# Gated cross-attention and mixture of experts: order of the last maximum, the second products, the selections, a send and a gather at the joint of the two halves

## The reference, cut to what matters

```
x (2, 512, 128), ctx (2, 154, 128), 16 heads of 8
x = x + tanh(g_xattn) * attention(layernorm(x), ctx, ctx)   # causal: query q sees keys k <= q
x = x + tanh(g_ffn)   * moe(layernorm(x))

moe: probs = softmax(xt @ Wr)                # 1024 tokens, 8 experts
     topv, topi = top_k(probs, 2);  topv = topv / sum(topv)
     rank = cumsum(onehot(topi), axis=0)     # per choice and expert, in token order
     keep = (rank <= 160) * onehot           # capacity of an expert for each choice
     h = gelu(xt @ W1[e] + b1[e]);  y = h @ W2[e] + b2[e]    # 128 -> 512 -> 128
     out = sum over e of w[t, e] * y[e, t]
```

## Time and profile before

| | us |
|---|---|
| median of 3 runs | 141.88 (141.72 to 141.99) |
| the profiled execution | 142.43 |
| its span, first to last instruction | 140.2 |
| busy: PE, DVE, POOL, ACT | 122.2, 103.5, 83.6, 74.1 |

### The profile page before, as it was taken

One profiled execution on the slowest core, in us unless ns is written; L12 is line 12 of the kernel. 1 busy time (PEld: TensorE's weight loads), 2 busy tenths in 40 slices (PEclk: granted clock), 3 DMA queues, 4 the chain that ended last, 5 costly groups with the idle time before them and its releaser, 6 DMA issues.

```text
span 140.2 us, 2215 instructions
## 1 busy us (share of the span) xinstructions
PE 122.2 (87%) x698; PEld 85.1 (61%) x703; DVE 103.5 (74%) x262; ACT 74.1 (53%) x135; POOL 83.6 (60%) x125
## 2 busy tenths in 40 slices
PE   5998978999899999896989979969989999989920
PEld 2443844455455656633449647759889999967710
DVE  5599855947584637399569698793699999999290
ACT  4924667166361447335916397671697777811210
POOL 6679779999999140021678658760077877772000
PEclk9999999999999999999999999999999999999996
DMA  3899880003340000000079601113820001101805
GB/s 97 257 217 228 207 274 4 5 0 91 71 140 0 5 0 0 0 0 2 19 222 301 215 22 39 39 53 65 181 66 29 26 31 43 39 30 25 294 0 150
DMA packets 19017, 12.22 MB, mean 87 GB/s; under 512 B 3381, under 2 KB 16999, under 8 KB 19008
## 3 DMA queue, kind: packets, MB, share of 16 engines
q1 hardware_dynamic: 17344, 9.59, 26.7%
q0 software_dynamic: 1088, 1.86, 4.1%
q10 hardware_dynamic: 576, 0.66, 1.3%
HBM read 7.25 MB, written 5.06 MB: 88 GB/s over the span
## 4 chain that ended last, share of the span: by engine, by line
PE 27%; DVE 22%; POOL 17%; issue 15%; DMA 8%; ACT 6%; POOLq 2%; DVEq 0%; SPq 0%
PE turn L870 5%; POOL results L588 5%; DVE top L1319 5%; POOL slots L558 4%; DMA xn_all<-results 3%; PE turn L883 3%; PE av L926 3%; DVE shared L1621 3%; DMA X<-x 3%; POOL shared L479 2%; PE av L934 2%; PE turn L889 2%; DMA results<-p,result_of 2%; PE turn L1105 2%; PE sc L902 2%
## 5 line engine op out<-in xcount | busy, mean ns | idle before, releaser
L1319 DVE TENSOR_REDUCE top<-turn 128x3 fp32r<-128x462 f32 (+2 forms) x44 | 26.2, 606 | 13.6 <-PE turn L870 7.4
L588 POOL DMA_INDIRECT results<-p,result_of x18 | 19.9, 1103 | 13.6 <-DVE p L1604 8.4
L682 ACT ACTIVATE p_all<-sc 128x1024 f32<-128x1024 f32 x16 | 15.5, 1022 | 16.9 <-PE sc L902 16.9
L558 POOL DMA_INDIRECT slots<-rows,slot_of x16 | 18.6, 1164 | 9.3 <-issue 7.3
L870 PE MATMUL turn<-shared,q_all 128*128 128x462 f32 (+2 forms) x44 | 20.3, 468 | 2.3 <-DVE top L1319 0.8
L1196 PE MATMUL sc<-q_all,w_all 128*128 128x320 f32 x96 | 17.4, 320 | 1.1 <-issue 0.7
L756 ACT ACTIVATE late<-sc,B 128x320 f32<-128x320 f32 x32 | 14.9, 522 | 3.0 <-PE sc L1196 3.0
L1196 PEld LDWEIGHTS sc<-q_all,w_all 128*128 128x128 f32 x96 | 14.2, 188 | 2.2 <-issue 1.9
L870 PEld LDWEIGHTS turn<-shared,q_all 128*128 128x128 f32 x44 | 8.3, 189 | 11.2 <-ACT q_pack_all L645 3.8
L1621 DVE TENSOR_TENSOR shared<-late,shared 128x640 fp32r<-128x640 f32 x16 | 13.1, 821 | 0.3
L549 POOL TENSOR_SCALAR_AFFINE_SELECT p_all<-p_all 128x512 f32<-128x512 f32 x7 | 4.5, 644 | 9.5 <-ACT p_all L682 9.5
(11 more groups left out here) (252 smaller groups left out, 280.5 us busy)
## 6 DMA issues: line engine op xcount, KB each, us to landing
W<-w SPq DMA_DIRECT2D x8, 256.0 KB, 3.2
p_all<-w SPq DMA_DIRECT2D x8, 256.0 KB, 4.4
slots<-slot SPq DMA_DIRECT2D x1, 1386.0 KB, 10.6
results<-zeros SPq DMA_DIRECT2D x2, 512.0 KB, 9.3
parts_all<-slots SPq DMA_DIRECT2D x5, 198.0 KB, 3.0
X<-x SPq DMA_DIRECT2D x2, 256.0 KB, 3.6
xn_all<-results SPq DMA_DIRECT2D x2, 256.0 KB, 4.1
xn_all<-results ACTq DMA_DIRECT2D x2, 256.0 KB, 4.3
```

The costliest lines, as they stand in the source:

```text
L558: nc.gpsimd.indirect_dma_start(out=slots, out_offset=bass.IndirectOffsetOnAxis(ap=slot_of[:, c:c + 1], axis=0), in_=rows[:, t, :], in_offs ...
L588: nc.gpsimd.indirect_dma_start(out=results, out_offset=bass.IndirectOffsetOnAxis(ap=result_of[0:m, e, n:n + 1], axis=0), in_=y[0:m, e % 2, ...
L682: act.activation(p0[:, t, heads, :], sc[:, heads, :], ACT.Exp, scale=SCALE).then_inc(sc_free, 1)
L1319: dve.tensor_reduce(top[:, qt, h0:h0 + nh, 3 * HD], ps[:, 0:nh * keys].rearrange("p (h k) -> p h k", h=nh), AX.X, ALU.max).then_inc(turn_f ...
```

## The change

At g = 5 and 6 VectorE reads the last maximum before `choose(0)`, and TensorE does `project_first` and `count(0)` after `values`. The three selections of the first batch each move to an earlier place on VectorE. GpSimd sends seven of the first batch's eight pieces before `root(blocks[1], 4)` and the eighth after it. `gather_on_chip(2, 0)` moves from behind `turn_results(0)` to behind `count(1)`; it uses `turn[1]` now, and the banks of later experts swap with it; the fills around it shrink from 4 and 8 to 2 and 4.

```
-        SELECTED = {(0, 0): 1, (1, 0): 2, (0, 1): 3, (1, 1): 5, (2, 0): 6, (2, 1): 7}
+        SELECTED = {(0, 0): 1, (1, 0): 2, (2, 0): 3, (0, 1): 4, (1, 1): 6, (2, 1): 7}
...
-            return ((sc1, av)[e] if e < ON_CHIP else turn[e % 2])[:, 0:SLOTS]
+            return ((sc1, av)[e] if e < ON_CHIP else turn[(e + 1) % 2])[:, 0:SLOTS]
...
-            for t in range(QT):
+            for t in range(QT - 1):
                 send(0, t)
+            send(0, QT - 1, range(TOPK - 1))
             root(blocks[1], 4)
+            send(0, QT - 1, range(TOPK - 1, TOPK))
...
                 maxima(maxima_beside(g, 3))
+                if g == 1:
+                    pe.wait_ge(v_ready, 5)
+                if 1 <= g <= NG:
+                    values(g - 1)
                 if g == FIRST_TURNED:
                     for h in range(2):
                         project_first(h)
                 if g == FIRST_PLACED:
                     count(0)
-                if g == 1:
-                    pe.wait_ge(v_ready, 5)
-                if 1 <= g <= NG:
-                    values(g - 1)
...
                 if e == ON_CHIP:
-                    pe.wait_ge(turn_free, full[0])
+                    pe.wait_ge(turn_free, use_of["fold", 2])
...
-            fill(sc[:, 3, :], 4)
+            fill(sc[:, 3, :], 2)
             count(1)
-            fill(sc[:, 0, :], 8)
+            gather_on_chip(2, 0)
+            fill(sc[:, 0, :], 4)
...
-                ps = turn[e % 2]
+                ps = turn[(e + 1) % 2]
...
             turn_results(0)
-            gather_on_chip(2, 0)
             gather_on_chip(2, 1)
...
-                if g == FIRST_TURNED:
+                if g == FIRST_PLACED:
                     choose(0)
-                if g == FIRST_PLACED:
                     dve.wait_ge(rstd_ready, 3)
                     scale_difference(0)
                     layernorm(blocks[0], x1, rows, rows_ready)
                     place(0)
+                    select_rows(0, 0)
                 if g == NG - 1:
                     last_later_keys()
-                    select_rows(0, 0)
+                    select_rows(0, 1)
                     low_of_rows(0, *blocks[0])
...
-            select_rows(0, 1)
+            select_rows(0, 2)
             choose_last()
...
             select_rows(1, 1, 2, QT)
-            select_rows(0, 2)
             split_hidden(0, (0,))
```

## The result

The changed kernel takes 141.19 us (median of 14 runs, 140.36 to 141.43); the kernel before, run beside it, took 142.14 (median of 14). The ratio is 0.9922, 95% interval 0.9901 to 0.9943, so 1.1 us faster (0.8 to 1.4). A kernel has a fast and a slower state on the chip, and every ratio here compares fast runs with fast runs, which in experiment 1 are only 6 of 12. The forecast was 2.1 us; rival 1 had 1.05. The profiled execution took 141.06 us, its span is 139.1 (before 142.43 and 140.2).

A forecast was written before the change was run, and what follows sets the result against it. Bound: the second root behind the sends. TensorE's path -0.90 - 1.26 = -2.16 and the load's -0.90 - 1.25 = -2.15 us; taken as 2.1, 142.43 gives 140.3 profiled, 139.8 median; range 139.3 to 141.8.

The forecast's parts named there:

- rival 1: Sends before the second root: fifth blocked behind the third selection, root 0.23 us late, gain 1.05, median 140.8; chance 0.26.
- What bounds the kernel: Second batch's root behind eight sends sets the expert stage's start; TensorE also pays 1.26 us for third expert's first gather.
- Products behind the values, maximum first: Early TensorE and VectorE: projection at 58.48 to 58.64, first places 0.29 to 0.62 us late, 1.31 us stall gone unused.
- Seven sends ahead of the root: GpSimd before the second root: bare gain 1.27 us; root at 77.59, VectorE going on 0.9 us earlier.
- First: blocked to 68.06 + d, ends 68.98 + d.: First send of the first batch: held by the first selection until 68.06 + d, then done at 68.98 + d.
- d: Lateness of the first places on VectorE, 0.29 to 0.62 us, taken as 0.45.
- the second case of rival 1: First send's extra 0.25 us stays and throws the second send behind the second selection, with the same effect.
- a margin of 0.1 us: Fifth send starts at 73.42 + d, ahead of the third selection at 73.52 + d.
- both start times carry the same d: Reason given against rival 1: the send's and the selection's starts are late by the same amount.
- The eighth send: GpSimd behind the second root: runs 78.97 to 79.94, and the second batch's sends don't wait for it.
- The load's path: Load before the first result send: 0.90 and 1.25 us earlier, 2.15 in sum.
- rival 5: Third selection waits 0.87 us for the fifth send; the first gain is zero, 1.26 left, median 140.6; chance 0.04.

The follow-up runs named there:

- experiment 1: The kernel before with one edit, seven sends, the root, then the eighth send: ratio 0.9917 to the kernel before.
- experiment 2: The changed kernel with all eight sends ahead of the root again: ratio 1.0079 to the kernel before.
- experiment 5: The changed kernel with six sends before the root instead of seven: ratio 0.9830 to the kernel before.
- experiment 3: The changed kernel with the third expert's first gather back behind the first result's turning, fills 4 and 8: ratio 1.0026 to the kernel before.
- experiment 4: The changed kernel with choice ahead of the last maximum and projection and count ahead of the values again: ratio 0.9829 to the kernel before.
- experiment 12: The changed kernel with the projection ahead of the values (last maximum still ahead of the choice) and six sends before the root: ratio 0.9822 to the kernel before.
- experiment 11: experiment 4's kernel with third selection back, five sends before the root, second count between gathers, third expert's first gather just before first result's turning: ratio 0.9932 to before.
- experiment 6: The changed kernel with only the projection back ahead of the values: ratio 0.9873 to the kernel before.
- experiment 9: experiment 4's kernel with one small clear on GpSimd ahead of the first send: ratio 0.9810 to the kernel before.
- experiment 7: The changed kernel with one small VectorE clear moved to just ahead of the second selection: ratio 0.9912 to the kernel before.
- experiment 8: The changed kernel with three small VectorE clears of an unused tile ahead of the second selection: 141.12 us in one execution.

## Why the prediction was wrong

**What bounds the kernel** was right: the root behind the sends (experiments 1, 2 and 5), and TensorE's 1.26 us of gather (experiment 3, 1.1 to 1.2).

**Products behind the values, maximum first.** Projection at 58.56 (forecast 58.48 to 58.64), places late by 0.40 (0.29 to 0.62, taken 0.45), the mask's cost moved to the choice's comparison (63.66, 0.67 us), last values at 70.08 waiting 1.02 us for VectorE (forecast 70.12). These came as written.

**The step that failed** is in "Seven sends ahead of the root": "First: blocked to 68.06 + d, ends 68.98 + d." It ended at 69.63, 1.17 us behind the first selection's end (68.46) and not 0.92: the first send's extra 0.25 us, visible in the earlier trace rows as 1.22 against 0.97, doesn't vanish while it is blocked. That put the second send's start at 69.93, behind the second selection's 69.86 (forecast 69.97 = 69.52 + d; d came out at 0.40 and the mask was 0.06 us shorter, but at 69.92 it would have been in front as well). From there on it went as the second case of rival 1 has it, root at 78.82 against its 78.86. I had both facts in hand and weighted 0.44 against 0.26 on a margin of 0.1 us, which is the fifth send's; the second send's margin in the sum was 0.24 us (69.28 + d against 69.52 + d), less than the 0.25 that stayed. My reason against the rival, "both start times carry the same d", was false: experiment 4 shows 0.42 and 0.26, because the selection hangs on TensorE as well.

That rival 1's total also fits (0.9922 of 141.88 is 140.8) is partly luck. It had the root 0.23 us late, and the first expert's last gather was 0.39 late; it had the gain at the first result send at 1.05, and that send came 1.71 us earlier.

**The eighth send** was costed at nothing. It runs beside the second placing (80.09 to 81.11) and holds a comparison of 0.17 us to 0.39; it ends with the send. That is 0.2 us of the 0.39 lost at the first expert.

**"The first result send comes 2.1 us earlier and eighteen sends carry it to the end"** was wrong too, and would have cost something even in the good case. The first was 1.71 us earlier (100.37 against 102.08), but the seventh waits 1.51 us for VectorE (109.72), which came only 0.89 earlier to the third expert's results (108.34 against 109.23). Before, that wait happened to end when the sends did, so it showed no idle. Experiment 12 says the same: its first result send is 0.83 us behind experiment 4's, and its last starts 0.03 us before. So the end follows VectorE and TensorE, and the last result send is only 0.63 us earlier (125.23 against 125.86). The load's path, forecast 2.15 us earlier, gained 0.64: its queue began at 94.38 against 95.02.

**Who waits for whom.** A send begun inside a selection is held (69.93, 2.25 us), but the selection of 73.93, begun inside the send of 73.78, takes its 1.48 us. A small comparison begun inside a send is held as well (80.71, 0.39 us), so rival 5's mechanism exists, only on another operation than the one I tested it on. The Trainium skill (page "SBUF — State Buffer", section "SBUF: two separate sides") says that whichever of the two operations starts first gets the shared pair of ports for the whole instruction and the other fully blocks. For selections against sends these runs bear that out one way only.

## What to carry to other kernels

Where a queue of GpSimd sends meets long two-input VectorE operations, work out the two start times of each meeting; where they are within 0.1 us of each other, the forecast is a coin and the schedule is fragile. Rather than aim for the lucky order, move the dependent step ahead of one more send, so that the order doesn't matter (experiment 5), and watch what waits for the sends themselves: in experiments 11 and 12 it was the load. An edit that frees an engine upstream can undo a lucky order downstream: the edit of the head removed 1.31 us of TensorE's stall and cost 1.3 us.

## What the runs showed of the hardware

A send that begins behind the start of a selection ends 0.92 us after the selection, the first of a row 1.17 us (the changed kernel, 69.63 behind 68.46). Of the others, one that started 0.07 or 0.08 us behind took 2.25 us (the changed kernel, experiment 6); one that started 0.09 us ahead took 1.02 or 1.03 us (experiments 4 and 9); one 0.06 us ahead was held and took 2.33 us (experiment 7). That the last had begun inside a clear doesn't explain it, since experiment 8's had too and took 0.98 us; that the 0.06 us were too short is the likely reading, from one trace.

Behind an idle of 2.17 us ahead of the first expert TensorE ran at half clock for a while, which cost 0.85 us (experiment 2); an idle of 1.10 us there was followed by none. But behind a stall of 1.31 us, earlier in the kernel, the clock fell in experiment 11's trace and not in that of the kernel before, so the length of the last idle alone doesn't decide it.
